# Attention and routed experts on one core: one list of 39 expert tiles instead of two lists with 46, and another order in the first quartet

## The reference

```python
x = x + attention(layernorm(x), ctx, ctx, mask)    # 16 heads of 8
h = layernorm(x)                                   # 2048 tokens
p = softmax(h @ wg.T)                              # 8 experts
top_w, top_i = top_k(p, 2); top_w /= sum(top_w)
y = sum over the 2 chosen e of top_w * (silu(h @ w1[e].T) * (h @ w3[e].T)) @ w2[e].T
out = x + y
```

## Time and profile before

| | us |
|---|---|
| median of 3 runs (lowest, highest) | 299.11 (298.17, 303.82) |
| profiled execution, its own time | 301.1 |
| its span, first to last instruction | 299.3 |
| busy: PE, DVE, ACT, POOL | 225.5, 219.7, 139.2, 114.3 |
| mean granted clock of TensorE | 0.871 of full |

### The profile page before, as it was taken

One profiled execution on the slowest core, in us unless ns is written; L12 is line 12 of the kernel. 1 busy time (PEld: TensorE's weight loads), 2 busy tenths in 40 slices (PEclk: granted clock), 3 DMA queues, 4 the chain that ended last, 5 costly groups with the idle time before them and its releaser, 6 DMA issues.

```text
span 299.3 us, 5642 instructions
## 1 busy us (share of the span) xinstructions
PE 225.5 (75%) x1522; PEld 171.6 (57%) x1522; DVE 219.7 (73%) x636; ACT 139.2 (47%) x312; POOL 114.3 (38%) x125
## 2 busy tenths in 40 slices
PE   0666888999899789795678664886889983999700
PEld 0643565667566557563366333775869973898500
DVE  5689965886688777969776831788788880788963
ACT  6684156655764474331445461543345550555300
POOL 5202150405030521053863540055367656443650
PEclk9996599999999999788557965999799996899965
DMA  7954513451344124426021333212123344253107
GB/s 214 339 189 99 132 29 79 94 115 34 70 98 82 35 47 93 83 59 208 10 63 45 68 76 83 58 31 73 37 68 88 81 84 102 64 157 103 37 11 211
DMA packets 40862, 27.31 MB, mean 91 GB/s; under 512 B 5214, under 2 KB 38501, under 8 KB 40448
## 3 DMA queue, kind: packets, MB, share of 16 engines
q1 hardware_dynamic: 37440, 20.95, 29.7%
q0 software_dynamic: 2816, 5.27, 5.9%
q10 hardware_dynamic: 576, 0.72, 0.8%
HBM read 13.27 MB, written 7.37 MB: 69 GB/s over the span
## 4 chain that ended last, share of the span: by engine, by line
PE 41%; DVE 22%; DMA 17%; SPq 8%; issue 7%; POOL 2%; ACT 1%; POOLq 1%; DVEq 0%
SPq L413 7%; PE bank L500 7%; DVE m_neg L1317 5%; DMA ys<-big 5%; DMA xg<-st_hi,rows_i 4%; DMA bd<-st 3%; PE bank L693 3%; PE bank L640 3%; PE bank L719 3%; PE bank L619 3%; PE bank L657 3%; PE bank L643 3%; PE bank L696 3%; PE bank L694 3%; PE bank L506 2%
## 5 line engine op out<-in xcount | busy, mean ns | idle before, releaser
L1009 POOL DMA_INDIRECT ys<-big x46 | 45.2, 982 | 38.3 <-DMA ys<-big 18.3
L1317 DVE TENSOR_REDUCE m_neg<-bank 128x4 f32<-128x512 f32 x64 | 43.3, 683 | 15.6 <-PE bank L657 15.2
L887 ACT ACTIVATE big<-bank 128x512 f32<-128x512 f32 x64 | 37.5, 597 | 23.5 <-PE bank L643 23.3
L761 ACT ACTIVATE st<-bank 128x128 fp32r<-128x128 f32 (+1 forms) x92 | 26.3, 329 | 35.3 <-PE bank L706 19.6
L970 POOL DMA_INDIRECT xg<-rows,rows_i x24 | 24.0, 1000 | 27.5 <-DVE rows_i L1173 12.4
L657 PE MATMUL bank<-bd,st 128*128 128x512 f32 x64 | 29.6, 499 | 6.4 <-DMA bd<-st 5.2
L640 PE MATMUL bank<-m_bd,ones_b 128*128 128x512 f32 x64 | 32.2, 504 | 2.4 <-ACT big L887 1.9
L1263 DVE SCALAR_TENSOR_TENSOR st<-st_hi,cst,bank 128x512 fp32r<-128x512 f32 x32 | 23.4, 748 | 9.2 <-ACT st_hi L761 4.5
L719 PE MATMUL bank<-bd,st 128*128 x92 | 27.5, 320 | 2.3 <-DVE big L1353 2.1
L987 POOL TENSOR_TENSOR m_bd<-mT,cst 128x512 fp32r<-128x512 f32 x16 | 17.2, 1109 | 30.1 <-DVE mT L1242 30.1
L922 ACT ACTIVATE big<-bank 128x256 f32<-128x256 f32 x46 | 17.7, 385 | 22.0 <-PE bank L696 21.8
(11 more groups left out here) (159 smaller groups left out, 538.0 us busy)
## 6 DMA issues: line engine op xcount, KB each, us to landing
bd<-st SPq DMA_DIRECT2D x128, 64.0 KB, 2.0
big<-xg SPq DMA_DIRECT2D x46, 64.5 KB, 1.9
raw<-in_L_ffn_w SPq DMA_DIRECT2D x2, 1024.0 KB, 9.0
raw<-ys SPq DMA_DIRECT2D x6, 256.0 KB, 4.6
xg<-in_patterns SPq DMA_DIRECT2D x18, 64.5 KB, 3.4
x_all<-in_x SPq DMA_DIRECT2D x4, 256.0 KB, 3.9
rows<-in_mask_BxS_if POOLq DMA_DIRECT2D x4, 256.0 KB, 4.9
ctx_all<-in_L_ffn_w SPq DMA_DIRECT2D x1, 1024.0 KB, 6.0
```

The source lines that it names most:

```text
L761: return nc.scalar.activation(o, i, ACT.Copy)
L887: nc.scalar.activation(prob[n % 2][:, NJ * g:NJ * (g + 1), :].rearrange("p h q -> p (h q)"), s2[k % 2][:, :], ACT.Exp, scale=SCALE).then_i ...
L1009: pool.indirect_dma_start(ys[f], bass.IndirectOffsetOnAxis(xt[n % XR][:, D:RW].bitcast(I32), 0), y_sb[n % YR], None, bounds_check=2 * CAPS ...
L1317: nc.vector.tensor_reduce(m_neg[:, H * (b - 1) + NJ * g:H * (b - 1) + NJ * (g + 1)], s1[k % s1_ring(u)][:, :].rearrange("p (j q) -> p j q" ...
```

## The change

One region per expert for all four quartets (`xg`, `ys` are single tensors). The number of tiles is that of 4096 pairs in 8 experts at most, 39. The first 17 in the list are full tiles of the first three quartets, since at least 17 full ones exist once these are routed; they need no pads. The other 22 are, per expert, the tiles begun but not among the 17, and those of the last quartet (`other_tiles`); pads are written once, ahead of these. Part 3 of the first table notes where each expert stands. The results of quartets 0 to 2 are loaded when 31 writes have landed.

In the expert stage the steps of quartet 3 start earlier: heads, projection and statistics of batch 15 ahead of the first tile, "x2T", "lg", "rk", "cn" at tiles 1, 3, 6, 8 instead of 5, 7, 10, 12, and sends in pairs after tiles 4 to 7. A write waits for the one two before it up to tile 16 and four before it from tile 17, the last ones too. All gathers stand behind the loop.

In the first quartet context values come ahead of the transposes, key stacks ahead of query stacks, the rest of the keys' context ahead of that of the tokens, the broadcast `ones_b` later; and GpSimd issues two of the four transfers for batch 0's keys.

```diff
-PHASES = (3, NQ - 3)
-CAPS = [n * T for n in PHASES]
-NTS = [(2 * c - E) // CT + E for c in CAPS]
-NT = sum(NTS)
-NC = CAPS[0] // CT
-REGS = [c + CT for c in CAPS]
+ROUTED = 2 * (NQ - 1) * T
+FULL_TILES = (ROUTED - E * (CT - 1) + CT - 1) // CT
+FIRST_TILES = (ROUTED - E) // CT + E
+NT = (2 * B * S - E) // CT + E
+NTS = (FULL_TILES, NT - FULL_TILES)
+NC = B * S // CT
+REG = B * S + CT
...
-C_TRI, C_ALL, C_BASE, C_FULL, C_UPTO, C_IDS, C_TILE = 344, 472, 600, 616, 632, 696, 696 + 2 * B
-C_N = C_TILE + NTS[0]
+C_TRI, C_ALL, C_BASE, C_FULL, C_UPTO, C_IDS, C_STEP, C_TILE = 344, 472, 600, 608, 632, 888, 888 + 2 * B, 904 + 2 * B
+C_N = C_TILE + NT
...
+    order = [("V", 0), ("xT", 0)]
     for u in range(NQ):
-        order += [("V", u)]
         if u:
-            order += [("MT", u - 1)]
+            order += [("V", u), ("MT", u - 1)]
...
+def stacks(u):
+    return sorted(STACKS, reverse=True, key=lambda s: s[0]) if u == 0 else STACKS
...
-            engine.wait_ge((kbd_ready if k else qbd_ready)[n % 3], 16 * NJ * (n // 3 + 1))
+            engine.wait_ge((kbd_ready if k else qbd_ready)[n % 3], 16 * NJ * (n // 3 + 1) - (32 if k and n % 3 == 0 else 0))
+            if k and n == 0:
+                engine.wait_ge(first_half, 32)
...
-                for j in range(NJ):
+                for j in range(2 if k and n == 0 else NJ):
...
+            def fill_pads():
+                sp.wait_ge(pad_ready, 1)
+                sp.dma_start(xg[E * REG:E * REG + CT, :], consts[:, C_PAD:C_PAD + RW]).then_inc(padded, 16)
+                _, at = nc.values_load_multi_w_load_instructions(pad[0:1, :], [mybir.EngineType.SP], min_val=0, max_val=E * REG - CT,
                                                                  skip_runtime_bounds_check_because=IN_RANGE)
                 for row in at:
-                    sp.dma_start(xg[f][bass.ds(row, CT), :], consts[:, C_PAD:C_PAD + RW]).then_inc(padded[f], 16)
+                    sp.dma_start(xg[bass.ds(row, CT), :], consts[:, C_PAD:C_PAD + RW]).then_inc(padded, 16)
+            def open_phase(f):
+                if f:
...
-                sp.wait_ge(padded[f], 16 * (E + 1))
+                if f:
+                    sp.wait_ge(padded, 16 * (E + 1))
...
+            def results_back(count):
                 for k in range(YR):
-                    sp.wait_ge(ysb_out[k], 16 * ((sum(NTS[0:f + 1]) - 1 - k) // YR + 1))
-            results_back(0)
+                    sp.wait_ge(ysb_out[k], 16 * ((count - 1 - k) // YR + 1))
+            results_back(FIRST_TILES)
...
+                if u >= 1:
+                    context_values(u)
...
-                    if k == 0:
+                    if k == 0 and u == 0:
+                        pe.wait_ge(ws_ready, 2)
+                    if not is_k and g == 0:
                         taken(pe, ("xT", u))
...
+            context_values(0)
             transpose_tokens(0)
...
+            heads_by_query(B - 1)
+            heads_by_dim(B - 1)
+            project_out(B - 1)
...
-                if n < 3:
-                    (heads_by_query, heads_by_dim, project_out)[n](B - 1)
-                if n == 5:
+                if n == 1:
                     fill(("x2T", NQ - 1))
-                if n == 7:
+                if n == 3:
                     fill(("lg", NQ - 1))
-                if n == 10:
+                if n == 6:
                     fill(("rk", NQ - 1))
-                if n == 12:
+                if n == 8:
...
-            for g in range(NG):
-                next_tokens(0, g)
+            next_tokens(0, 3)
+            next_tokens(0, 1)
...
+            take_normalised(B - 1)
...
-                if n == 1:
-                    take_normalised(B - 1)
-                if n == 5:
+                if n == 2:
...
+            stacks_in(pool, 0, 1)
+            pool.wait_ge(bd_cleared, 3)
+            for j in range(2, NJ):
+                rows = slice(R * j, R * (j + 1))
+                pool.dma_start(bd_slot(1, 0)[rows, :, j, :].bitcast(F32), st[rows, 0, 1, :, 0:S].bitcast(F32)).then_inc(first_half, 16)
...
-                if 2 <= n < NT - 6:
-                    pool.wait_ge(ysb_out[(n - 2) % YR], 16 * ((n - 2) // YR + 1))
...
+                back = 2 if n < NTS[0] else 4
+                if n >= back:
+                    pool.wait_ge(ysb_out[(n - back) % YR], 16 * ((n - back) // YR + 1))
...
+                if n == 4:
...
-                if 8 <= n < 8 + 4 * QB and n % 2 == 0:
-                    send(QB * (NQ - 1) + (n - 8) // 4, n // 2 % 2)
+                if 4 <= n < 4 + QB:
+                    for k in range(2):
+                        send(QB * (NQ - 1) + n - 4, k)
...
+            def ones_b_columns():
+                nc.vector.tensor_copy(ones_b[:, :, :], cst[:, C_BATCH:C_BATCH + QB].unsqueeze(2).to_broadcast([P, QB, P])
+                                      ).then_inc(setup_ready, 1)
+            def context_rest(u):
+                dve.wait_ge(ckhi_ready, u + 1)
+                nc.vector.tensor_tensor(ck_lo[:, :], ck[:, :], ck_hi[:, :].bitcast(F32), ALU.subtract).then_inc(cklo_ready, 1)
...
+                if part == 3:
+                    own(nc.vector.tensor_tensor(until[:, :], until[:, :], tiles[:, :], ALU.subtract))
+                    own(nc.vector.tensor_scalar(until[:, :], until[:, :], -1.0, float(n), ALU.mult, ALU.add))
+                    own(nc.vector.scalar_tensor_tensor(tiles[:, :], until[:, :], 0.0, tiles[:, :], ALU.max, ALU.min))
+                    tiles_of(begun[:, :], 0, 3 * T // CT, ALU.is_gt)
+                    own(nc.vector.tensor_tensor(group[:, 0, :], begun[:, :], tiles[:, :], ALU.subtract))
+                    own(nc.vector.scalar_tensor_tensor(origin[:, 0:E], tiles[:, :], float(CT), base, ALU.mult, ALU.add))
+                    own(nc.vector.scalar_tensor_tensor(origin[:, E:2 * E], begun[:, :], float(CT), base, ALU.mult, ALU.add))
...
+            def other_tiles(part):
+                n = NTS[1]
+                number = cst[:, C_TILE:C_TILE + n]
+                groups = group[:, :, :].rearrange("p k e -> p (k e)")
+                below = x2s[1][:, 0:4 * E * E].rearrange("p (m f) -> p m f", f=2 * E)
+                passed, moved = (x2s[k][:, 0:n * 2 * E].rearrange("p (n m) -> p n m", m=2 * E) for k in range(2))
+                spot, column = (line[:, k * n:(k + 1) * n] for k in range(2))
+                if part == 0:
+                    counts(1)
+                    nc.vector.tensor_tensor(pad[:, :], cnt[:, :], base, ALU.add).then_inc(pad_ready, 1)
+                    tiles_of(tiles[:, :], 0, NC, ALU.is_gt)
+                    own(nc.vector.tensor_tensor(group[:, 1, :], tiles[:, :], begun[:, :], ALU.subtract))
+                    own(nc.vector.tensor_tensor(below, groups.unsqueeze(1).to_broadcast([P, 2 * E, 2 * E]), upto, ALU.mult))
+                    own(nc.vector.tensor_reduce(ended[:, 1:2 * E + 1], below, X, ALU.add))
+                if part == 1:
+                    own(nc.vector.scalar_tensor_tensor(origin[:, :], ended[:, :], -float(CT), origin[:, :], ALU.mult, ALU.add))
+                    own(nc.vector.tensor_tensor(step[:, :], origin[:, 1:2 * E + 1], origin[:, 0:2 * E], ALU.subtract))
+                    own(nc.vector.tensor_tensor(passed, ended[:, 1:2 * E + 1].unsqueeze(1).to_broadcast([P, n, 2 * E]),
+                                                number.unsqueeze(2).to_broadcast([P, n, 2 * E]), ALU.is_le))
+                    own(nc.vector.tensor_tensor(moved, passed, step[:, :].unsqueeze(1).to_broadcast([P, n, 2 * E]), ALU.mult))
+                    own(nc.vector.tensor_reduce(spot, moved, X, ALU.add))
+                if part == 2:
+                    own(nc.vector.tensor_tensor(moved, passed, cst[:, C_STEP:C_STEP + 2 * E].unsqueeze(1).to_broadcast([P, n, 2 * E]), ALU.mult))
+                    own(nc.vector.tensor_reduce(column, moved, X, ALU.add))
+                    own(nc.vector.tensor_copy(tab[:, 1, NTS[0]:NT], column))
+                    own(nc.vector.scalar_tensor_tensor(spot, number, float(CT), spot, ALU.mult, ALU.add))
+                    nc.vector.tensor_scalar(tab[:, 0, NTS[0]:NT], spot, origin[:, 0:1], float(E * REG), ALU.add, ALU.min).then_inc(tab_ready, 1)
...
+            context_rest(0)
             split_tokens(0)
+            ones_b_columns()
...
+            normalise_heads(B - 1)
+            take_projection(B - 1)
+            second_statistics(NQ - 1)
...
-                    normalise_heads(B - 1)
-                if n == 2:
-                    take_projection(B - 1)
-                if n == 3:
-                    second_statistics(NQ - 1)
-                if n == 4:
                     normalise(QB * (NQ - 1), 2 * NQ - 1)
-                if 8 <= n < 11:
-                    routing_step(NQ - 1, n - 8)
-                if n == 11:
+                if 4 <= n < 6:
+                    routing_step(NQ - 1, n - 4)
+                if n == 6:
+                    routing_step(NQ - 1, 2)
+                if n == 8:
```

(8 more changed lines are left out.)

159 lines of the change are left out of this document (81 added, 78 removed).

## The result

| | before | changed |
|---|---|---|
| median of 4 runs (lowest, highest), us | 298.97 (298.17, 303.82) | 290.55 (289.48, 291.24) |
| ratio of the runs, 95% interval | 1 | 0.9724 [0.968, 0.977] |
| profiled execution, its span | 301.1, 299.3 | 289.48, 287.7 |

The ratio leaves out the 303.82 of before, which lies more than 1.5% above the lowest. The change makes the kernel 2.8% faster, 8.4 us; 17.6 were predicted, so 281.5 missed by 9.05. Of this, 3.0 us are only which executions were profiled: the one before lay 2.0 over the forecast's median, the changed one 1.1 under its own. Against its own profiled run the sum gave 283.5 and the run took 289.48. **6.0 us have to be found in the trace**, at 281.7 against 287.7 of span.

A forecast was written before the change was run, and what follows sets the result against it. No single engine bounds the kernel; the expert stage is long, at VectorE's pace plus a boundary gap. hidden(0) at 182.97 plus 98.7 gives 281.7 us of span, 17.6 less; 299.11 - 17.6 = 281.5 us, range 276 to 288.

The forecast's parts named there:

- the shorter list: Expert stage: 46 tiles become 39, hidden(0) to hidden(38) 61.2 us plus VectorE's extra work and the boundary.
- the routed rows: Expert stage: the last quartet's routed rows ready at +23.6 us from hidden(0), against +30.5 before.
- the sends: GpSimd's queue: the last quartet's row transfers in pairs, 4.2 us a pair, last one landed at +40.9 us.
- the boundary: Between the list's two parts: hidden(16) at +43.5 us, with 6 us of gap staying.
- the 22 steps after it: Expert stage after the boundary: 38.1 us from hidden(16), so hidden(38) at +81.6.
- did not close: Rival at the boundary: it closes, tile 16 near +40, time about 277 us; chance 0.15.
- the rival of GpSimd's landings: GpSimd's queue: landings stay at 4.4 us to tile 16, pairs take 5.1, time about 286 us; chance 0.20.
- a sign of being wrong: Boundary: the forecast is wrong if tile 17 waits for the pads or the table and not the sends.
- Start of the stage: Ahead of the first tile: pads leave, saving 1.4 us, 0.8 kept after VectorE's new work; ends 0 and 1.4.
- First quartet: Attention's start: first maximum 1.3 us sooner, less 0.3 for larger constants, net 1.0; ends -0.3 and 2.5.
- The drain: Expert stage's end: 5.0 us from the last hidden to VectorE's last result, at +86.6.
- The tail: Kernel's end: last write at +88.0, twelve gathers of 7.9 us covered until +93.5, span ends at +98.7.

The follow-up runs named there:

- e3: e1 with TensorE's second table read also moved ahead of tile 17's transpose, against the changed kernel: 290.10 us.
- e9: The changed kernel run again, unaltered, on a slower chip: 300.67 us, ratio to before 0.9605.
- e1: Changed kernel with TensorE's first table read moved into the last attention quartet: 291.50 us.
- e5: Changed kernel with table rows 64 entries wide and the second part at entry 32, as in the kernel before: 296.83 us, ratio to before 0.951.
- e14: The kernel of e11 run again, on a third chip: 282.04 us, ratio to before 0.938.
- e7: Changed kernel with its first-quartet part undone, constants still large: 299.34 us, ratio to before 0.9602.
- e12: Repeat of e7, beside the changed kernel e9: 298.88 us.
- e10: Changed kernel with VectorE's clearing of the second value buffer moved ahead of the first quartet's stacks: 298.91 us, ratio to before 0.9554.
- second and third comparison: Runs e5 to e8 and e9 to e12, on one slower chip; the kernel before took 311.23 and 312.72 us there.
- e6: Changed kernel with the constants loaded in two parts, the rest behind the gate's weights: 300.03 us, ratio to before 0.9653.
- e8: e5 plus the last quartet's eight sends together behind tile 4's write and the table's steps one tile earlier: 294.43 us.
- e11: Changed kernel plus wide table, split constants, early clearing, sends together, earlier table steps, second read before tile 17, weights and first combination in the drain: 292.39 us.

## Why the prediction was right and wrong

**Right.** The faster kernel and the way to it: the shorter list, the routed rows, the sends, the boundary and the 22 steps after it: hidden(38) came at +81.45 for +81.6. The gap moved and did not close, as predicted. Its shape was off: 3.87 us of stand for 5 to 7, since tiles 6 to 15 ran slower than I had them. Writes stood 7.0 us in all for landings, not 20, and the rival of GpSimd's landings did not occur: sends and writes landed with a median of 2.6, the slowest in 5.8 and 5.4. One thing came close unseen: I had SyncE's read of the table done at about +37, and it ended at +40.7, 0.9 us before the last send landed. In e3 and on the chip of e9 it ended last, and tile 17 waited for the table, which the prediction had named as a sign of being wrong.

**Start of the stage (failed): most of the 3.3 us at hidden(0).** From the landing of tile 0's load to hidden(0) it was 0.6 us before and is 4.2 now, 3.6 more, where I had kept 0.6 as lost; that misses by 3.0. From the third quartet's routing to that landing 0.7 more was gained than forecast (2.1 for 1.4), and the first quartet missed by 1.0: the third quartet's rows were routed at 164.23, as before (164.24), and not 1.0 sooner. "I keep 0.8 of the 1.4" weighed VectorE's new work and never asked what else stands between project_out(15) and the first transpose. There stands TensorE's register read. Before, TensorE made it while it waited for the sends. The change puts the heads of batch 15 ahead of it, shortens the sends, and packs the table so that the read starts at byte 156 of its row in the SBUF. e1 shows that the read goes where it is put, e5 that the packing makes it 2.7 us longer. With the table wide the read lies beside the tile's load: of the 3.0 us from the load's landing to the transpose, e5 keeps 0.04 and e14 0.49. I had priced the second read at 0.5, by its extra values; the first at nothing, and the end that I gave this term, the whole 1.4 lost, did not reach it either.

**First quartet, 1.0 (mis-sized; in part open).** At one moment of the clock's rise the part is worth 0.9 to 1.0 (e7, e12 on the line above), for 1.3. The profiled execution had its clock up 2.5 us later than the one of before, 1.2 us by the line's slope, and the larger constants moved the first statistics from 4.84 to 5.29. Whether that later rise is chance or belongs to the new order no run separates. That the key stacks could run at half clock was in neither my term nor its range, though the earlier trace rows lay beside it. The scores' lead over the clearing, 1.5 us, was named in the prediction and had been there to take (e10).

**The drain, 0.9.** I took 5.0 us from the last hidden to the last result and it was 6.1: 6.3 before. So the gathers that stood in it before made it at most 0.2 longer. TensorE waits for VectorE's result before it starts the next tile's `down`, and VectorE waits for that: the last result stood 1.02 for it, in both kernels alike (the second of the earlier trace rows).

**The tail, 1.8 (failed).** "twelve are 7.9 us, from about +83 to +91, covered by the last write's landing and the last loads (until +93.5)". They stand behind the loop in VectorE's program, so they could not start before the last result at +87.5, nor at +83 by the prediction's own +86.6 for it. They ran from 274.17 to 282, and the last four, ready to go at 280.8, waited for them. My own text gave the sign: it is wrong if VectorE still gathers rows of the first quartets when the last loads land. The last write at +90.2, not +88.0, cost nothing for the same reason.

**The rest, 3.0**, is which execution was profiled. One profiled run each way is worth no more than that here; the forecast of 281.5 leaned on a difference of 2.0 that the changed kernel's profiled run had with the other sign.

## What to carry to other kernels

Work that "is covered" needs a start time: look where it stands in its own engine's program before giving it a slot. Look on the sequencer's rows too, not only at busy time: an "issue" stand ahead of a dynamic slice can be a register read, and where a table begins can cost more than how long it is. When an edit is worth less than a microsecond, compare the same events inside traces at the same moment of the clock's rise, and steps at the same granted clock, since totals can't tell. And when an edit shortens two things, read each from its own stand before putting the total down to one.

## What the runs showed that was not expected

**Register reads and where they start.** By the start in bytes from the beginning of the table in its partition: 0, 128, 224, 256, 384 took 1.5 to 2.1 us for 17 or 22 values, 192 took 2.9 for 31; 68 and 156 took 4.2 to 4.8, in every trace. The starts with the short reads are all multiples of 32 bytes; the two others are multiples of 4 and not even of 8. Nine starts (320, with 15 values in 1.7 us, is the ninth) suggest that alignment decides, and leave open whether to 8, 16 or 32 bytes; starts in between were not tried. The Trainium skill, in "Runtime: NRT & Kernel Launch", section "Instruction fetch mechanics", gives some 200 ns a register, for reads from HBM; these are reads from the SBUF, and of 17 or 22 values the long ones come to 210 to 270 ns a value, the short ones to 75 to 95.

**A stand on one chip.** On the chip of the second and third comparison, the traces of e5, e6, e7, e9, e10 and e12 have 11 to 13 us between hidden(12) and hidden(13), where the others have about 3. Timelines of TensorE and of SyncE's queue in e9:

```profile
223.87 0.57 PE L746 MATMUL bank<-bd,st 128*128 x1 [5.17 <-issue]
```
```profile
217.04 14.58 SPq L453 DMA_DIRECT2D xg<-in_patterns  x8
```

The eight pad transfers took 14.58 us there and 6.08 in the changed kernel's first trace, and several engines stood at once for "issue". SyncE's slow read of the table was on the path in each of the five that have the narrow table, and of the traces without the stand only in e3. e8 and e11, whose pads and sends are placed otherwise, had 6.5 and 5.0 us at tile 24 instead. The kernel before took 12 us more on this chip too. What it is was not tried: it stays open.
